# Three scores and a key sum moved into the projections between two attention units

## The reference, cut to what matters

```python
x = L0_attn_x                                    # (16, 1024, 256), float32
x = x + attn(layernorm(x))
x = x + ffn(layernorm(x))

# attn: 8 heads, two score maps each, D = 16
q = rope(x @ Wq.T) * scaling;  k = rope(x @ Wk.T);  v = x @ Wv.T
probs = softmax(q @ k.T)                         # 16 maps of 1024 x 1024 a sequence
diff = probs[:, :, 0] - lam * probs[:, :, 1]
attn = diff @ v                                  # then an RMS norm per head, and @ Wo.T

# ffn: scan over the 16 x 1024 rows, reshaped by sequence
c = sigmoid(x wf + c uf + bf) * c + sigmoid(x wi + c ui + bi) * tanh(x wc + c uc + bc)
h = tanh(x wo + c_final uo + bo)
```

## Time and profile before

| what | value |
|---|---|
| median of 3 runs | 5033.72 us (5031.82 to 5034.27) |
| profiled execution | 5053.02 us, span 5051.2 us |
| mean granted TensorE clock | 0.986 of full speed |
| PE busy | 4895.6 us, 97% |
| DVE busy | 3960.6 us, 78% |
| ACT busy | 2884.9 us, 57% |
| POOL busy | 2930.4 us, 58% |

### The profile page before, as it was taken

The page is one execution under the profiler, slowest core; times in us unless marked ns, Lnnn a source line. Parts: engine busy times, 40 slices in busy tenths (PEclk is TensorE's granted clock), DMA queues, the critical chain, the costliest instruction groups (busy, mean ns, idle before and its releaser), DMA issues.

```text
span 5051.2 us, 67243 instructions
## 1 busy us (share of the span) xinstructions
PE 4895.6 (97%) x24784; PEld 1745.4 (35%) x24784; DVE 3960.6 (78%) x6295; ACT 2884.9 (57%) x5221; POOL 2930.4 (58%) x2134
## 2 busy tenths in 40 slices
PE   7999999999999999999999999999999999999999
PEld 2224242332424233242332424233242433324237
DVE  7888878888887878878887887888788787887526
ACT  1565646656465665646566464665646566564642
POOL 3583837657374674728567383764738477472740
PEclk7899999999999999999999999999999999999999
DMA  6121222303122130222313123230312313022117
GB/s 151 30 56 52 47 66 53 66 32 66 47 47 72 34 76 38 55 59 47 72 34 62 46 47 70 48 66 30 67 48 47 72 34 76 39 47 55 68 51 291
DMA packets 127867, 311.19 MB, mean 62 GB/s; under 512 B 27313, under 2 KB 30514, under 8 KB 113714
## 3 DMA queue, kind: packets, MB, share of 16 engines
q1 hardware_dynamic: 124562, 289.72, 24.1%
q10 hardware_dynamic: 2976, 17.17, 0.9%
HBM read 172.07 MB, written 99.61 MB: 54 GB/s over the span
## 4 chain that ended last, share of the span: by engine, by line
PE 77%; POOL 11%; ACT 5%; DVE 3%; issue 3%; DMA 0%; SPq 0%; ACTq 0%; DVEq 0%; POOLq 0%
PE s_ps L795 15%; PE o_ps L835 15%; PE st L822 14%; PE st L928 13%; POOL pair_sum L484 11%; PE sum_ps L850 7%; PE st L763 4%; PE st L781 4%; ACT probs L591 3%; DVE neg_max L1127 2%; PE st L1005 2%; PE st L906 1%; PE o_ps L750 1%; DVE xa L1114 1%; PE s_ps L1005 1%
## 5 line engine op out<-in xcount | busy, mean ns | idle before, releaser
L484 POOL TENSOR_TENSOR pair_sum<-probs 128x512 f32<-128x512 f32 x2048 | 2822.1, 1414 | 1211.3 <-ACT probs L591 1210.6
L1127 DVE TENSOR_REDUCE neg_max<-s_ps 128x1 f32<-128x512 f32 x4096 | 2582.1, 682 | 700.2 <-PE s_ps L795 697.8
L591 ACT ACTIVATE probs<-st 128x512 f32<-128x512 f32 x4096 | 2162.3, 603 | 971.6 <-PE st L822 810.6
L795 PE MATMUL s_ps<-k_stack,q_stack 96*128 96x512 bf16 x4096 | 1523.0, 389 | 43.5 <-DVE neg_max L1127 37.0
L822 PE MATMUL st<-q_stack,k_stack 99*128 99x512 bf16 x4096 | 1475.8, 385 | 28.7 <-ACT probs L591 7.5
L835 PE MATMUL o_ps<-probs,values 128*32 128x512 f32 x8192 | 1095.3, 607 | 12.2 <-ACT probs L591 8.5
L822 PEld LDWEIGHTS st<-q_stack,k_stack 99*128 99x128 bf16 x4096 | 368.3, 97 | 1360.1 <-ACT probs L591 905.2
L795 PEld LDWEIGHTS s_ps<-k_stack,q_stack 96*128 96x128 bf16 x4096 | 400.7, 98 | 686.0 <-DVE neg_max L1127 336.6
L850 PE MATMUL sum_ps<-pair_sum,ones 128*32 128x512 f32 x4096 | 534.9, 594 | 26.6 <-POOL pair_sum L484 26.6
L928 PE MATMUL st<-pair_sum,weights 128*128 128x512 f32 x768 | 381.9, 594 | 11.8 <-ACT pair_sum L547 11.8
L541 ACT ACTIVATE probs<-st,gate_bias 128x512 f32<-128x512 f32 x192 | 131.7, 686 | 441.7 <-PE st L928 441.7
(11 more groups left out here) (151 smaller groups left out, 2926.6 us busy)
## 6 DMA issues: line engine op xcount, KB each, us to landing
q_stack<-qk_parts SPq DMA_DIRECT2D x384, 128.0 KB, 4.3
k_stack<-qk_parts SPq DMA_DIRECT2D x381, 128.0 KB, 7.0
swapped<-xa SPq DMA_DIRECT2D x128, 256.0 KB, 2.4
qk_parts<-swapped SPq DMA_DIRECT2D x64, 512.0 KB, 2.8
qk_parts<-low_part SPq DMA_DIRECT2D x64, 256.0 KB, 3.0
probs<-in_x SPq DMA_DIRECT2D x16, 1024.0 KB, 9.7
x_rows<-probs SPq DMA_DIRECT2D x16, 1024.0 KB, 3.9
xa<-in_x SPq DMA_DIRECT2D x15, 1024.0 KB, 6.0
```

What stands on the lines that cost most here:

```text
L484: pool.tensor_tensor(pair_sum[q % 2][:, h, :], probs[a % 4][:, h, :], probs[(a + 1) % 4][:, h, :], ALU.add)\
L591: act.activation(probs[kk % 4][:, h, :], st[n % BANKS][:, :], ACT.Exp).then_inc(exp_done, 1)
L795: pe.matmul(s_ps[i % BANKS][:, :], q_stack[g][0:SROWS, s, t * P:(t + 1) * P], k_stack[g][0:SROWS, s, h * HALF:(h + 1) * HALF], start=True, ...
L1127: dve.tensor_reduce(neg_max2[:, at, i % 2:i % 2 + 1], s_ps[i % BANKS][:, :], AX.X, ALU.max, negate=True).then_inc(max_done, 1)
```

## The change

Three scores of unit u + 2 (`MIDDLE = 3`) are issued among the passes of the queries' projection, one behind each of its second, third and fourth matmul. Key sum 15 comes between the queries' and the keys' passes. DVE takes the three maxima ahead of `finish_sums`. `PLAN1` starts at score 3, and the extra work of 2 and 3 in its steps 0 and 1 is gone. The edit acts in the 15 iterations that aren't the last.

```diff
+MIDDLE = 3
...
-WORK[1][0] += 2
-WORK[1][1] += 3
...
-PLAN1 = score_plan(0, SCORES - sum(LATE), 1)
+PLAN1 = score_plan(MIDDLE, SCORES - sum(LATE), 1)
...
-            def qk(g, b, ab, blocks=iter(()), each=(1,) * 8):
-
-                for X in range(2):
+            def qk(g, b, ab, blocks=iter(()), each=(1,) * 8, parts=(0, 1)):
+
+                for X in parts:
...
                 turn_max(u + 1)
                 if not last:
-                    qk(1, b, ab)
+                    qk(1, b, ab, ((u + 2, 0, i) for i in range(MIDDLE)), (0, 1, 1, 1, 0, 0, 0, 0), (0,))
                 key_sums(u, 0, 15)
+                if not last:
+                    qk(1, b, ab, parts=(1,))
                 if not last:
                     pe.wait_ge(act_out, ab + QK1 + 4)
                 attention(u + 1, 1, u + 2, NO_PLAN if last else PLAN1)
...
                 split_shift(u + 1)
+                if not last:
+                    for i in range(MIDDLE):
+                        maximum(u + 2, i)
                 finish_sums(u, 0, 3)
```

## The result

The changed kernel takes 5042.73 us (median of 17 runs, 5040.79 to 5047.53), the kernel before 5033.72 on the same chip: ratio 1.0018, 95% interval 1.0011 to 1.0024. It is 9 us slower, inside the range and just inside the 0.2% that I had called no change. I had forecast +2.3, a ratio of 1.0005, which lies outside the measured interval: the miss of 7 us is real.

A forecast was written before the change was run, and what follows sets the result against it. PE was taken as the bound, except a stretch of the second unit where POOL sets the time. +1.75 up to there and −1.60 behind give +0.15 us an iteration, +2.3 in all on 5033.7: forecast 5036, range 5020 to 5058.

The forecast's parts named there:

- Key tile +1.46: Second unit's first key tile, later by 1.46 us: 0.66 for three scores, 0.80 for the now uncovered last copy.
- Ramp +0.62: First key tile to first weighted sum: seven scores instead of three, 3.57 us instead of 2.95.
- Front −0.33 behind the ramp: First intervals after the ramp: three scores become four (+0.13), then five become four (−0.46), then equal.
- POOL's stretch: Steps 5 to 14: POOL sets the time; its start moves by +1.75 us, its length stays, a lighter plan gains nothing.
- Rival A: PE's savings count everywhere, also in steps 8 to 14: −0.4 to −1.3 us an iteration, about 5022 us; chance 0.22.
- Behind it −1.60: After step 14's key sum: three intervals go from five scores to four (−0.46 each), one from three to two (−0.22).
- Rival B: Ramp is DVE's, backlog lasts into next steps: +1.0 to +1.4 us an iteration, 5049 to 5055; chance with D 0.14.
- Rival C: Second unit's rotary steps collide with POOL at the SBUF port: 5056 to 5110 us; chance 0.14.
- D: Score 0 waits long for `shift_made` or the stacks, nothing gained: +1.2 us, 5052; chance with rival B 0.14.
- The own time: Kernel before: profiled 5053.0 us less 19.8 for four long rotary steps gives 5033.2; median 5033.7 taken as base.

The follow-up runs named there:

- keysum_only: Kernel before with only key sum 15 moved between the queries' and keys' passes, no scores in the passes, extra work kept; ratio to before 1.0027.
- eleven_plan: Kernel before with another plan only: one score more in steps 7, 11, 12 and 27, one less in 14, 21, 24 and 29; ratio 0.9964.
- best_plan: Kernel before with another plan only: one score more in steps 7 and 10, two in 20, one less in 14, 21, 24, 29; ratio 1.0013.
- late_fill: As best_plan, but two scores added in steps 11 and 12 instead of 7 and 10; ratio to the kernel before 0.9971.
- fill_stretch: Kernel before with another plan only: one score more in steps 7, 10, 11, 12, one less in 14, 21, 24, 29; ratio 1.0015.
- keysum_back: Changed kernel with key sum 15 back behind the keys' passes, scores in the passes and new plan kept; 5098.78 us, ratio to before 1.0111.
- fill_more: fill_stretch with one score more in steps 6, 8 and 9, one less in 17, 22 and 25; ratio to the kernel before 0.9976.
- plan_only: Kernel before with only the extra work in steps 0 and 1 gone, all 96 scores in the attention; 5117.23 us, ratio 1.0142.

## Why the prediction was right, and where it was mis-sized

The mechanism and nearly every interval came as worked out. The path should have been +0.15 us an iteration and was +0.57. Both are small differences of a loss up to the key sum of step 14 (+1.75 forecast, +1.88 measured) and a gain behind it (−1.60 forecast, −1.32 measured). The range was wide against the net, so that the total fell into it proves little; the terms are the test. The 0.42 us between are these terms:

1. *Key tile +1.46, measured +1.61.* The three scores cost 0.66 and the copy 0.85, as said. What I left out is the first pass behind the key sum: eight passes take 3.54 us from 1468.16 to the end of the last slot (0.2 before ACT's start at 1471.90), 0.1 more than 8 × 0.43, and the key sum stands 0.30 instead of 0.22 behind the score. keysum_only has the first of these alone: 10.94 for 9.98.
2. *Ramp +0.62, measured +0.56.* Right, down to the seventh score's wait.
3. *Front −0.33 behind the ramp*: 2.85, 2.85, 2.85, 3.49 came to the hundredth.
4. *POOL's stretch*: predicted to take what it took. From the first weighted sum to the key sum of step 14 it is 39.83 against 40.11, −0.28, where −0.33 of front should have come: POOL's third pair starts 0.33 earlier, and from there on the stretch takes 0.04 more. Rival A, that PE's savings count everywhere, fell, though this run tests it little: steps 5 to 13 hold at most two scores in either plan, and below two nothing is saved anyway. The experiments show that the wall isn't POOL's alone: two scores more in steps 7 and 10 of the kernel before, and DVE sets a later time.
5. *Behind it −1.60, measured −1.32.* Two times 0.46 and the one at step 14 came. The interval of two scores at step 15 took 2.52 and not 2.40: ACT has a cast of 1.08 us between its exponentials there and runs without a gap; and at step 20 the key sum came 0.19 late, because the new plan puts five scores in step 18 and DVE takes these maxima ahead of its sums. That is the step of the prediction that failed: "All other intervals keep their counts or have a key sum and another limit". The count was kept, the limit was DVE, and DVE's order had changed. The prediction had also misread the plans: it said that the change takes three of seven five-score steps out, but it takes five (2, 14, 21, 26 and 29) and adds one, step 18, the very step that delays DVE.

Together 0.15 − 0.06 + 0.05 + 0.28 = 0.42 us. I had said that I was wrong if the second unit wasn't 95.7 us long: it was 95.99, and by that sign the gain was mis-sized, as told under 5. Rival B (backlog beyond the ramp) didn't come in the changed kernel; with key sum 15 back it came in full and dearer than priced, 4.0 us an iteration over before in the mean. Rival C didn't come in the profile of the changed kernel. D didn't: score 0 had no wait.

The own time was read rightly: without its four long rotary steps the profile of before gives 5033, the median.

## What to carry to other kernels

Count what one more instruction costs in each interval of a periodic schedule, from starts in the trace; here 0 to 2 scores cost nothing, the third and fourth 0.22 us and the fifth 0.46, and this table told most intervals of the study to some hundredths wherever PE set the time (the two beside step 20 were 0.21 and 0.58 off). Work moved to a new place pays only if it leaves a full interval and lands in a free one: the change moved three scores to where each costs 0.22 too and took the cover off a copy to make it possible, while another plan alone (eleven_plan) saved 1.21 us an iteration. And before another engine's wait is called free time, look at what that engine has queued: two maxima ahead of DVE's sums cost 1.24 us (best_plan), two between them nothing (late_fill), all four 1.69 (fill_stretch).

## What the runs showed of the hardware

A wait of PE can cost twice: behind it the granted clock may fall to the lower level, 1.2 GHz, for some microseconds (0.57 on average over 3.3 us in the fence of keysum_back, 0.50 over 3 us in that of fill_stretch). It fell behind the wait of 2.45 us in all 15 iterations of keysum_back, behind 1.90 us in 6 of 15 (best_plan), behind 1.72 us in 7 of 15 (fill_stretch), behind 1.31 us in 1 of 15 (fill_more), and never behind the 0.69 us of the naked copy. So the length of the wait alone doesn't decide it; a fall cost 1.1 us in fill_stretch and best_plan.

A VectorE operation with two SBUF inputs can wait for more than one of GpSimd's. Rotary steps of 6.20 instead of 1.26 us, four additions longer, stand in seven of the thirteen profiled kernels, at the same place of the first unit, in 1 to 6 of 15 iterations, though that unit's program is the same in all; plan_only has two of 9.49 us in its second unit. The Trainium skill, SBUF — State Buffer, section "Who interferes with whom", has the loser blocked for the winner's whole instruction; here the measurement says it can be blocked for the winner's next ones too: the step of 6.20 us in iteration 4 of the kernel before and one of the 9.49 us both end 1.08 us behind the last of an unbroken row of additions. In the profiled executions four such steps go with 20 us of longer first units, six with 34. That they are also why the kernel before runs from 5031 to 5040 us on one chip and from 5037 to 5070 on another is likely but not shown, and why a chip should have more of them stays open; no run was made to settle it.
